# Row maxima of causal attention: 32x32 block transposes on VectorE and eight small transfers per half, in place of TensorE transposes

## The chip, the cores and the metric

One core of one Trainium2 chip runs the whole program. The metric is the device time of one execution in microseconds (us); lower is better. The engines are PE (TensorE, matrix products; PEld is its weight load), DVE (VectorE), ACT (ScalarE), POOL (GpSimd) and SP (SyncE, which here only issues DMA transfers). "ACTq" and "SPq" are DMA issues on the queues of ACT and SP.

## The reference, cut to what matters

The input has 32 sequences of 376 tokens (375 and one of padding) with 256 features. Three layers follow one another: a token mixer (a causal filter of 32 taps and two projections), causal attention with 16 heads of 16 features, and a mixture of experts. Only the attention is touched:

```python
q = (x @ wq + bq).reshape(b, s, h, hd).transpose(0, 2, 1, 3)
k = (x @ wk + bk).reshape(b, s, h, hd).transpose(0, 2, 1, 3)
...
scores = jnp.einsum('bhqd,bhkd->bhqk', q, k) / jnp.sqrt(jnp.float32(hd))
scores = jnp.where(causal, scores, -jnp.inf)
weights = jax.nn.softmax(scores, axis=-1)
attn = jnp.einsum('bhqk,bhkd->bhqd', weights, v)
```

The softmax subtracts, for each query and head, the largest score of its row. The change is about how that maximum gets from where it is found to where it is used.

## The kernel before

**Three phases.** The attention phase works through 32 sequences and takes about the first 1320 us. The routing phase and the pages phase (the experts) follow; the change doesn't touch them.

**A step.** The attention phase is software-pipelined: step b attends to sequence b, finds the row maxima of sequence b+1, makes queries and keys (the "front") for sequence b+2, mixes b+3 and finishes b-1. A step has 28 units, n = 0 to 27, in four groups of heads (g = n // 7); half 0 of the heads are units 0 to 13, half 1 units 14 to 27. In each unit PE makes one bank of scores with queries on the partitions (for the maxima of sequence b+1, line 584) and one with keys on the partitions (for the exponentials of sequence b, line 618). Between them it does the dense products of the step, each at a unit written out by hand: `hid` at 1 and 2, `nT` at 9 and 10, q at 13 and 14, k at 17 and 18, `out` at 22 and 23, `conv` at 24 and 25, `val` at 6 and 27. Every engine runs its own program in its own order and waits on semaphores. A dense product lies in one of two banks, taken in turn; the next but one product waits until ACT (`take_hi`) and DVE (`take_lo`) have read it.

**The way of the maxima.** DVE reduces each bank of scores along the keys and writes minus the maximum to `neg_max` (line 830), queries on the partitions. The second pass has keys on the partitions and queries along the columns, and wants the maximum inside the product: `k_rows` holds two rows of ones, and `q_rows` gets two rows with the high and the low part of minus the maximum, so that the product comes out as score minus maximum. So the maxima must be turned:

- `max_T` (PE): three transposes per half (line 566) of `neg_max`, 8 heads by 376 queries, into a dense bank. Half 1 is turned at unit 5 of the next step, half 0 at unit 20.
- `take_hi` (ACT, unit 5 or 20) writes the high part, `take_lo` (DVE, unit 6 or 21) the low part, to `maxT`, 8 rows of 376.
- `max_rows` (SP, line 1088): four transfers per half, each of four rows of 1504 B, from `maxT` to the one row of `q_rows` that it fills.
- `open_exp` (PE): unit 0 waits until half 0 has landed in `q_rows`, unit 14 until half 1 has.

**SP's order in a step:** `max_rows` of half 1; the rows of half 0 of q (8 transfers) and k (6), waiting for q and k of this step; `max_rows` of half 0; `store` (2); `load_x` (2, waits for `conv1`); the rows of half 1 of q (8, waits for the exponentials of unit 27) and k (6). SP issues one after another.

**Clears.** At units 9 and 11 ACT issues one transfer each of 816 KB of zeros to DRAM (`x_sorted`, `y_sorted`; line 746), which the phases behind need.

Of the kernel before, what the change touches and what calls it, by code (L numbers as in the profile page):

```python
# [24 lines left out]
F32 = mybir.dt.float32  # L25
# [8 lines left out]
P = 128  # L34
# [60 lines left out]
def attention_phase(nc, sem, sh, front, experts, h2_dram, x_sorted, y_sorted, pages_cleared,  # L95
# [7 lines left out]
    ROWS = 3 * sh.HD  # L103

    with ExitStack() as ctx:
# [44 lines left out]
        q_rows = [sb(f"q_rows{p}", [P, 8, S], F32R) for p in range(2)]  # L150
# [3 lines left out]
        maxT = [sb(f"maxT_{s}", [8, 2, S], F32R) for s in ("hi", "lo")]  # L154
# [28 lines left out]
        max_taken = sem("max_taken")  # L183
        exp_scores = sem("exp_scores")
# [42 lines left out]
        with nc.Block() as block:  # L227
# [75 lines left out]

            @block.tensor
# [88 lines left out]
        DENSE = 16  # L393

        class Step:
# [14 lines left out]
            @staticmethod  # L410
            def names(b):

                mix, front, maxima, attend, finish = (0 <= b + d < B for d in (3, 2, 1, 0, -1))
                return (["hid0", "hid1"] * front + ["maxT1"] * attend + ["val0"] * maxima
                        + ["nT0", "nT1", "q0", "q1", "k0", "k1"] * front + ["maxT0"] * maxima
                        + ["out0", "out1"] * finish + ["conv0", "conv1"] * mix + ["val1"] * maxima)
# [60 lines left out]
        with nc.Block() as block:  # L477

            @block.tensor
            def _(eng):  # L480
# [80 lines left out]
                def max_T(st, half, shift):  # L561

                    ps = open_bank(st, f"maxT{half}")
                    eng.wait_ge(max_taken, st.at(shift, GROUPS * UNITS, 2 * UNITS * (half + 1)))
                    for t in range(NT):
                        last = eng.transpose(ps[0:8, t * P:t * P + T[t]], neg_max[0:T[t], t, half, :],
                                             ident[0:T[t], 0:T[t]])
                    close(last)

# [34 lines left out]
                def open_exp(st, g, u):  # L604
                    n = g * UNITS + u
                    if u == 0 and g % 2 == 0:
                        eng.wait_ge(max_loaded[st.b % 2][g // 2], st.turn(0, 64, 64))
# [54 lines left out]
                def step(st):  # L662
                    for n in range(GROUPS * UNITS):
# [10 lines left out]
                        if n == 5 and st.attend:  # L674
                            max_T(st, 1, 0)
# [8 lines left out]
                        if n == 20 and st.maxima:  # L684
                            max_T(st, 0, 1)
# [12 lines left out]
            def _(eng):  # L698
# [64 lines left out]
                def step(st):  # L763
                    opens = isinstance(st.i, int) and st.b == -2
                    for n in range(GROUPS * UNITS):
# [9 lines left out]
                        if n == 5 and st.attend:  # L775
                            take_hi(st, "maxT1", maxT[0][0:8, 1, :], 8)
# [19 lines left out]
                        if n == 20 and st.maxima:  # L796
                            take_hi(st, "maxT0", maxT[0][0:8, 0, :], 8)
# [5 lines left out]
            def _(eng):  # L803
# [3 lines left out]
                HI = ["maxT1", "nT0", "nT1", "q0", "q1", "k0", "k1", "maxT0", "conv0", "conv1"]  # L807
# [13 lines left out]
                def maxima(st, g, u):  # L821
# [8 lines left out]
                    eng.tensor_reduce(dst, src, AX.X, ALU.max, negate=True).then_inc(max_taken, 1)  # L830

# [60 lines left out]
                def step(st):  # L892
                    for n in range(GROUPS * UNITS):
# [7 lines left out]
                        if n == 6 and st.attend:  # L901
                            take_lo(st, "maxT1", maxT[1][0:8, 1, :], maxT[0][0:8, 1, :], 8)
# [13 lines left out]
                        if n == 21 and st.maxima:  # L916
                            take_lo(st, "maxT0", maxT[1][0:8, 0, :], maxT[0][0:8, 0, :], 8)
# [116 lines left out]
            def _(eng):  # L1034
# [15 lines left out]
                def rows(st, half, name):  # L1050
# [11 lines left out]
                    for c in range(2):  # L1062
                        for n, part in enumerate(order):
                            eng.dma_start(dst[par][64 * c + 16 * n:64 * c + 16 * n + 16, 4 * half:4 * half + 4, :]
# [3 lines left out]
                    if name == "q":  # L1068
                        for c in range(2):

                            at, slots = 64 * c + ROWS, slice(4 * half, 4 * half + 4)
                            eng.dma_start(q_rows[par][at:at + 2, slots, :].bitcast(F32),
                                          q_rows[par][at + 2:at + 4, slots, :].bitcast(F32)
# [6 lines left out]
                def max_rows(st, half, shift):  # L1080

                    par = (st.b + shift) % 2
                    _, k = st.product(f"maxT{half}")
                    eng.wait_ge(dense_read, k + 1)
                    for c in range(2):
                        for part in range(2):
                            row_ = 64 * c + ROWS + part
                            eng.dma_start(q_rows[par][row_:row_ + 1, 4 * half:4 * half + 4, :].bitcast(F32),
# [1200 lines left out]
```

## Time and profile before

| | |
|---|---|
| median of 3 runs | 2006.88 us (1999.67 to 2010.14) |
| profiled execution, first to last instruction | 2006.0 us |
| PE busy over the span | 1780.7 us, 89% |
| DVE busy over the span | 1414.0 us, 70% |
| ACT, POOL busy over the span | 1006.7 us, 1057.2 us |
| attention phase, first to last score product | about 58 to 1297 us |
| DMA packets over the span | 214515, 291.09 MB |

The profiled execution's record gives its span and no further time around it; it lies 0.9 us under the median of the runs. A busy share says how long an engine had something in it; since matrix products overlap in PE, a busy PE isn't at its peak. Idle time of an engine is put down to what ended it.

### The profile page before, as it was taken

The numbers are of one execution on the slowest core, as the hardware profiler recorded it, in microseconds if no ns is written. First come the engines' busy times: TensorE is split into PE (matmuls) and PEld (weight loads), VectorE is DVE, ScalarE is ACT, GpSimd is POOL, SyncE is SP. The second block draws the span as 40 slices with busy tenths as digits, with TensorE's granted clock in tenths as the row PEclk, the third lists the DMA queues.
The fourth block names the chain that finished last, engine by engine and source line by source line (L and its number), as shares of the span: only waits on it lengthen the run. The fifth ranks groups of instructions, "written<-read, shape, count | busy, mean of one in ns | idle before, by whom it ended". The sixth has DMA issues, their size and how long they took to land. (4 is left out here: it accounts for less than half of the span.)

```text
span 2006.0 us, 49812 instructions
## 1 busy us (share of the span) xinstructions
PE 1780.7 (89%) x14801; PEld 1389.7 (69%) x14802; DVE 1414.0 (70%) x3857; ACT 1006.7 (50%) x2112; POOL 1057.2 (53%) x1443
## 2 busy tenths in 40 slices
PE   4899999999999999999999998848889984988883
PEld 4667777777777777777777776447777774977773
DVE  3468788788788788788788787357888872355554
ACT  1156556556556556656656656532443431544441
POOL 4034555555555555555555554525667663266666
PEclk7689999999999999999999999768999997999997
DMA  2434343343334334334334333222333335799996
GB/s 74 75 111 138 121 131 136 121 129 137 120 128 138 120 126 140 120 125 141 120 125 142 119 113 136 67 82 84 117 108 125 111 112 157 236 329 325 325 317 222
DMA packets 214515, 291.09 MB, mean 145 GB/s; under 512 B 44854, under 2 KB 176666, under 8 KB 214426
## 3 DMA queue, kind: packets, MB, share of 16 engines
q1 hardware_dynamic: 178010, 186.11, 30.1%
q0 software_dynamic: 18048, 49.31, 7.7%
q10 hardware_dynamic: 18368, 54.64, 7.1%
q8 instruction: 38, 0.62, 0.1%
q14 instruction: 51, 0.42, 0.1%
HBM read 83.25 MB, written 129.69 MB: 106 GB/s over the span
## 5 line engine op out<-in xcount | busy, mean ns | idle before, releaser
L830 DVE TENSOR_REDUCE neg_max<-bank 120x1 f32<-120x376 f32 (+2 forms) x896 | 522.3, 596 | 215.5 <-PE bank L584 208.6
L739 ACT ACTIVATE probs<-bank 128x376 f32<-128x376 f32 (+2 forms) x896 | 454.7, 522 | 281.7 <-PE bank L618 270.6
L584 PE MATMUL bank<-k_rows,q_rows 64*128 64x128 f32 (+2 forms) x1536 | 412.0, 342 | 31.5 <-ACT probs L739 27.7
L618 PE MATMUL bank<-q_rows,k_rows 64*120 64x120 f32 (+2 forms) x1536 | 397.6, 343 | 4.2 <-ACT probs L739 4.2
L949 POOL TENSOR_SCALAR_AFFINE_SELECT probs<-probs 128x512 f32<-128x512 f32 (+1 forms) x384 | 233.9, 628 | 241.5 <-ACT probs L739 241.5
L601 PE MATMUL bank<-causal,own_row 64*120 64x120 bf16 (+4 forms) x1792 | 293.1, 244 | 12.1 <-DMA k_rows<-k_flat_hi 8.2
L584 PEld LDWEIGHTS bank<-k_rows,q_rows 64*128 64x128 f32 (+1 forms) x1536 | 240.9, 189 | 51.0 <-ACT probs L739 46.0
L2171 POOL DMA_INDIRECT y_got<-y_sorted,p_route x188 | 183.0, 973 | 122.1 <-issue 117.9
L1815 POOL DMA_INDIRECT x_sorted<-r_normed,route x188 | 183.8, 978 | 103.2 <-DVE route L1662 50.1
L618 PEld LDWEIGHTS bank<-q_rows,k_rows 64*128 64x128 f32 (+1 forms) x1536 | 230.5, 184 | 9.1 <-ACT probs L739 6.6
L601 PEld LDWEIGHTS bank<-causal,own_row 64*128 64x128 bf16 (+2 forms) x1792 | 149.8, 115 | 125.1 <-issue 56.0
L654 PE MATMUL bank<-probs,val 128*32 128x376 f32 (+2 forms) x3072 | 193.3, 385 | 2.6 <-POOL probs L949 2.6
L890 DVE RECIPROCAL recip<-sums 128x94 f32<-128x94 f32 x256 | 186.0, 729 | 0.1
L654 PEld LDWEIGHTS bank<-probs,val 128*32 128x32 f32 (+1 forms) x3072 | 88.7, 112 | 97.5 <-issue 73.1
L975 POOL TENSOR_TENSOR attn_raw<-attn_raw,recip 128x376 f32<-128x376 f32 x64 | 63.8, 996 | 144.7 <-DVE recip L890 144.7
L1364 PE MATMUL rbank<-shared_down,r_hidden 128*128 128x256 f32 x376 | 93.4, 391 | 28.2 <-DVE base L1518 28.2
L2129 DVE SCALAR_TENSOR_TENSOR base<-y_got,p_route,base 128x256 f32 (+1 forms) x94 | 41.4, 482 | 100.9 <-DMA y_got<-y_sorted,p_route 100.9
L1002 POOL TENSOR_TENSOR resid<-hid,bias_o 128x256 f32<-128x256 f32 (+1 forms) x96 | 67.7, 733 | 72.4 <-DVE out_rows L874 72.4
L2010 PE MATMUL pbank<-w_gate_up,xT 128*128 x816 | 105.5, 285 | 0.0
L2010 PEld LDWEIGHTS pbank<-w_gate_up,xT 128*128 128x128 f32 x816 | 99.4, 199 | 1.1 <-issue 0.5
L1364 PEld LDWEIGHTS rbank<-shared_down,r_hidden 128*128 128x128 f32 x376 | 67.8, 190 | 41.4 <-DVE base L1518 33.9
L955 POOL TENSOR_SCALAR var_eps<-moments 128x3 f32<-128x3 f32 x32 | 7.4, 233 | 167.1 <-DVE moments L850 167.1
(226 smaller groups left out, 4176.3 us busy)
## 6 DMA issues: line engine op xcount, KB each, us to landing
x_sorted<-zeros ACTq DMA_DIRECT2D x32, 816.0 KB, 4.0
y_sorted<-zeros ACTq DMA_DIRECT2D x32, 816.0 KB, 4.4
x_rows<-x_sorted SPq DMA_DIRECT2D x51, 512.0 KB, 6.2
y_sorted<-p_y_rows SPq DMA_DIRECT2D x51, 512.0 KB
q_rows<-q_flat_hi SPq DMA_DIRECT2D x256, 94.0 KB
k_rows<-k_flat_hi SPq DMA_DIRECT2D x248, 94.0 KB
q_rows<-q_flat_lo SPq DMA_DIRECT2D x128, 94.0 KB
out_dram<-base SPq DMA_DIRECT2D x47, 256.0 KB
```

Of the source, the lines that this page charges most:

```text
L584: last = eng.matmul(ps[0:T[t], m * w:(m + 1) * w], q[rows, slot, t * P:t * P + T[t]], k[rows, slot, 0:w], start=False, stop=(m == len(head ...
L601: eng.matmul(dst, own_row[group, h, 0:d], causal[group, h, 0:m, first:d], start=(h == 0), stop=False, skip_group_check=True)
L618: last = eng.matmul(ps[0:T[t], m * w:(m + 1) * w], k[64 * c:64 * c + 64, slot, t * P:t * P + T[t]], q[64 * c:64 * c + 64, slot, t * P:S], ...
L654: last = eng.matmul(bank_pv[32 * j:32 * j + 32, t * P:S], val[par][0:kk, t, 4 * (g // 2) + j, 32 * e:32 * e + 32], probs[g % 2][0:kk, j, O ...
L739: eng.activation(probs[g % 2][0:T[t], first:first + len(heads), OFF[t]:OFF[t] + w], bank_exp[n % 2][0:T[t], 0:len(heads) * w].rearrange("k ...
L830: eng.tensor_reduce(dst, src, AX.X, ALU.max, negate=True).then_inc(max_taken, 1)
L890: eng.reciprocal(recip[:, cols], sums[:, cols]).then_inc(recip_done, 1)
L949: eng.affine_select(out=blk, in_=blk, compare_op=ALU.is_ge, fill=0.0, base=0, pattern=[[0, 4], [1, d]], channel_multiplier=-1).then_inc(pr ...
L1364: last = eng.matmul(bank_y[t // 2][:, t % 2 * D:(t % 2 + 1) * D], hidden[c][:, t * P:(t + 1) * P], experts.down[:, c, :], start=(c == 0 an ...
L1815: eng.indirect_dma_start(x_sorted, at, normed[st.b % 4][:, t, :], None)\
L2010: last = eng.matmul(bank_gu[par][:, a * 2 * MR:(a + 1) * 2 * MR], xT[par][a // 2][:, k, a % 2 * P:(a % 2 + 1) * P], routed.gate_up[:, k, e ...
L2171: eng.indirect_dma_start(y_got[ring][:, t, k, :], None, y_sorted, at)\
```

## The change

The PE transposes, the copies by ACT and DVE, `maxT` and two of the 16 dense products of a step go. In their place DVE, after its own maximum of unit 0 (half 1) or unit 14 (half 0), writes the high and low parts of the maxima side by side into `max_parts`, 32 columns per query tile, and turns them in blocks of 32x32 into `max_turned`. A query's place is then (tile, block of 32, column in it), and the blocks of one tile lie on four groups of 32 partitions; so SP carries them to `q_rows` in eight transfers per half, each from 8 partitions to two rows, in runs of 32 numbers (128 B), 24 runs in each. `q_rows` grows from 376 to 384 columns. Half 0 is turned six units earlier than before, half 1 five units earlier. SP's order is unchanged.

```diff
-        q_rows = [sb(f"q_rows{p}", [P, 8, S], F32R) for p in range(2)]
+        q_rows = [sb(f"q_rows{p}", [P, 8, SPAN], F32R) for p in range(2)]
...
-        maxT = [sb(f"maxT_{s}", [8, 2, S], F32R) for s in ("hi", "lo")]
+        max_parts = [sb(f"max_parts{h}", [P, NT, 32], F32R) for h in range(2)]
+        max_turned = [sb(f"max_turned{h}", [P, NT, 32], F32R) for h in range(2)]
...
-        DENSE = 16
+        DENSE = 14
...
-                def max_T(st, half, shift):
-
-                    ps = open_bank(st, f"maxT{half}")
-                    eng.wait_ge(max_taken, st.at(shift, GROUPS * UNITS, 2 * UNITS * (half + 1)))
-                    for t in range(NT):
-                        last = eng.transpose(ps[0:8, t * P:t * P + T[t]], neg_max[0:T[t], t, half, :],
-                                             ident[0:T[t], 0:T[t]])
-                    close(last)
...
-                        eng.wait_ge(max_loaded[st.b % 2][g // 2], st.turn(0, 64, 64))
+                        eng.wait_ge(max_loaded[st.b % 2][g // 2], st.turn(0, 128, 128))
...
-                        if n == 5 and st.attend:
-                            max_T(st, 1, 0)
...
-                        if n == 20 and st.maxima:
-                            max_T(st, 0, 1)
...
-                        if n == 5 and st.attend:
-                            take_hi(st, "maxT1", maxT[0][0:8, 1, :], 8)
...
-                        if n == 20 and st.maxima:
-                            take_hi(st, "maxT0", maxT[0][0:8, 0, :], 8)
...
+                def turn_maxima(st, half, shift):
+
+                    parts = max_parts[half][:, :, 0:16].rearrange("q t (c s m) -> q t c s m", c=2, s=2)
+                    whole = neg_max[:, :, half, :].rearrange("q t (c m) -> q t c m", c=2)
+                    done = st.at(shift, 2, half + 1)
+                    eng.wait_ge(max_taken, st.at(shift, GROUPS * UNITS, 2 * UNITS * (half + 1)))
+                    eng.tensor_copy(parts[:, :, :, 0, :], whole).then_inc(max_hi, 1)
+                    eng.wait_ge(max_hi, done)
+                    eng.tensor_tensor(parts[:, :, :, 1, :], whole, parts[:, :, :, 0, :].bitcast(F32), ALU.subtract)\
+                        .then_inc(max_lo, 1)
+                    eng.wait_ge(max_lo, done)
+                    eng.transpose(max_turned[half][:, :, :].rearrange("q t i -> q (t i)").bitcast(F32),
+                                  max_parts[half][:, :, :].rearrange("q t i -> q (t i)").bitcast(F32)).then_inc(max_turns, 1)
...
-                        if n == 6 and st.attend:
-                            take_lo(st, "maxT1", maxT[1][0:8, 1, :], maxT[0][0:8, 1, :], 8)
+                        if n == 0 and st.attend:
+                            turn_maxima(st, 1, 0)
+                        if n == 14 and st.maxima:
+                            turn_maxima(st, 0, 1)
...
                 def max_rows(st, half, shift):
 
                     par = (st.b + shift) % 2
-                    _, k = st.product(f"maxT{half}")
-                    eng.wait_ge(dense_read, k + 1)
+                    wait_alone(eng, max_turns, st.at(shift, 2, half + 1), passed_sp)
                     for c in range(2):
-                        for part in range(2):
-                            row_ = 64 * c + ROWS + part
-                            eng.dma_start(q_rows[par][row_:row_ + 1, 4 * half:4 * half + 4, :].bitcast(F32),
-                                          maxT[part][4 * c:4 * c + 4, half, :].bitcast(F32)).then_inc(max_loaded[par][half], 16)
+                        rows_ = q_rows[par][64 * c + ROWS:64 * c + ROWS + 2, 4 * half:4 * half + 4, :].bitcast(F32)\
+                            .rearrange("s m (t b i) -> s m t b i", b=4, i=32)
+                        for b in range(4):
+                            eng.dma_start(rows_[:, :, :, b, :],
+                                          max_turned[half][32 * b + 8 * c:32 * b + 8 * c + 8, :, :].bitcast(F32)
+                                          ).then_inc(max_loaded[par][half], 16)
```

The rest of the diff clears `neg_max` and `max_parts` once at the start, adds three semaphores and drops the two names from the lists that number the dense products.

## Rows read from the trace of the kernel before

**Rows 1.** The page: span, and busy time of each engine

```profile
span 2006.0 us, 49812 instructions
...
PE 1780.7 (89%) x14801; PEld 1389.7 (69%) x14802; DVE 1414.0 (70%) x3857; ACT 1006.7 (50%) x2112; POOL 1057.2 (53%) x1443
```

**Rows 2.** Windows: stretch and length, busy by engine, PE clock, DMA share, GB/s

```profile
241.00:1184.00 943.00, 917.04 (x8750) 676.96 (x8748) 759.99 (x1625) 580.91 (x1225) 489.37 (x725) 1.00 0.39 128
```

**Rows 3.** Timeline of PE, units 5 to 9 of one step (start, length in us)

```profile
713.92 0.49 PE L566 MATMUL bank<-ident,neg_max 128*8 128x128 f32 x3
714.34 0.26 PE L601 MATMUL bank<-causal,own_row 64*120 64x120 bf16 x1
...
718.51 0.38 PE L584 MATMUL bank<-k_rows,q_rows 64*128 64x256 f32 x1 [0.54 <-ACT probs L739]
```

**Rows 4.** Timeline of ACT, unit 6 of the same step

```profile
716.42 1.58 ACT L714 ACTIVATE normed<-hid,row_shift_by,rstd 128x256 f32<-128x256 f32 x3 [0.22 <-POOL row_shift_by L963]
```

**Rows 5.** Waits from 200 to 1200 us: total, times, longest (us)

```profile
ACT normed L714 <- POOL row_shift_by L963: 6.5, 26, 0.3
...
PEld bank L515 <- DVE out_rows L874: 7.6, 25, 0.3
```

**Rows 6.** Timeline of POOL, unit 20 of the same step

```profile
734.91 0.64 POOL L949 TENSOR_SCALAR_AFFINE_SELECT probs<-probs 128x512 f32<-128x512 f32 x1 [1.38 <-ACT probs L739]
```

**Rows 7.** Groups of DVE: smallest operand, and the 32-partition shuffle

```profile
L1561 DVE TENSOR_TENSOR shifted<-top 128x8 f32<-128x8 f32 x23 | 3.6, 158 | 0.0
...
L884 DVE STREAM_SHUFFLE sums<-sums_swapped 128x376 f32<-128x376 f32 x64 | 37.6, 588 | 0.3
```

**Rows 8.** Timeline of DVE, the maximum of unit 2 in the next step

```profile
748.19 0.69 DVE L830 TENSOR_REDUCE neg_max<-bank 128x2 f32<-128x512 f32 x1 [0.77 <-PE bank L584]
```

**Rows 9.** Timeline of SP's queue, late part of the step

```profile
738.03 0.68 SPq L1088 DMA_DIRECT2D q_rows<-maxT_hi  x1
...
740.05 0.57 SPq L1088 DMA_DIRECT2D q_rows<-maxT_lo  x1
741.00 0.42 SPq L1104 DMA_DIRECT2D h_dram<-out_rows  x1
...
743.01 0.41 SPq L1045 DMA_DIRECT2D x_in<-in_x_dram  x1
...
745.10 1.29 SPq L1064 DMA_DIRECT2D q_rows<-q_flat_hi  x2
...
753.58 0.59 SPq L1064 DMA_DIRECT2D k_rows<-k_flat_hi  x1
```

**Rows 10.** Timeline of SP's queue near the end of the phase

```profile
1274.94 0.58 SPq L1088 DMA_DIRECT2D q_rows<-maxT_hi  x1
```

**Rows 11.** Transfers from 1274.5 to 1279.5 us, in 40 slices

```profile
GB/s 0 0 0 0 0 0 0 0 0 0 0 0 0 24 24 0 0 0 24 24 0 0 0 24 24 0 0 0 24 24 0 366 418 418 418 287 339 261 392 366
```

**Rows 12.** Timeline of PE: first exponential products of units 0 and 14

```profile
744.38 0.42 PE L618 MATMUL bank<-q_rows,k_rows 64*120 64x120 f32 x2
...
762.03 0.42 PE L618 MATMUL bank<-q_rows,k_rows 64*120 64x120 f32 x2
```

**Rows 13.** Timeline of ACT's queue: second clear of the same step

```profile
758.80 0.55 ACTq L746 DMA_DIRECT2D y_sorted<-zeros  x1
```

**Rows 14.** Transfers from 756.5 to 764.5 us: issues, size, us to landing

```profile
y_sorted<-zeros ACTq DMA_DIRECT2D x1, 816.0 KB, 4.4
```

**Rows 15.** Timeline of ACT's queue, step with the late rows

```profile
1244.75 0.54 ACTq L746 DMA_DIRECT2D y_sorted<-zeros  x1
```

**Rows 16.** Timeline of SP's queue in that step

```profile
1246.32 1.35 SPq L1088 DMA_DIRECT2D q_rows<-maxT_lo  x1
```

**Rows 17.** Timeline of PE in that step, unit 14

```profile
1250.26 0.33 PE L584 MATMUL bank<-k_rows,q_rows 64*128 64x128 f32 x1 [3.31 <-DMA q_rows<-maxT_lo]
```

**Rows 18.** Windows around an idle stretch of PE: columns as in rows 2

```profile
113.50:115.20 1.70, 0.04 (x1) 0.00 (x0) 1.38 (x4) 1.70 (x5) 1.37 (x3) 1.00 0.02 7
...
117.20:120.40 3.20, 3.20 (x28) 1.25 (x28) 1.52 (x4) 1.01 (x3) 0.00 (x0) 0.50 1.02 406
```

More of the change, by code:

```diff
@@ L103, in attention_phase @@
     ROWS = 3 * sh.HD
+    SPAN = NT * P
     with ExitStack() as ctx:
@@ L183, in attention_phase @@
         max_taken = sem("max_taken")
+        max_hi = sem("max_hi")
+        max_lo = sem("max_lo")
+        max_turns = sem("max_turns")
         exp_scores = sem("exp_scores")
@@ L302, in _ @@
                 eng.memset(moments[:, :, :], 1.0)
+                eng.memset(neg_max[:, :, :, :], 0.0)
+                for h in range(2):
+                    eng.memset(max_parts[h][:, :, :].bitcast(F32), 0.0)
             @block.tensor
@@ L413, in names @@
                 mix, front, maxima, attend, finish = (0 <= b + d < B for d in (3, 2, 1, 0, -1))
-                return (["hid0", "hid1"] * front + ["maxT1"] * attend + ["val0"] * maxima
-                        + ["nT0", "nT1", "q0", "q1", "k0", "k1"] * front + ["maxT0"] * maxima
+                return (["hid0", "hid1"] * front + ["val0"] * maxima
+                        + ["nT0", "nT1", "q0", "q1", "k0", "k1"] * front
                         + ["out0", "out1"] * finish + ["conv0", "conv1"] * mix + ["val1"] * maxima)
@@ L806, in _ @@
                 HALF_1_AT, HALF_0_AT = (10, 11, 12, 13, 16), (22, 24, 25, 26, 27)
-                HI = ["maxT1", "nT0", "nT1", "q0", "q1", "k0", "k1", "maxT0", "conv0", "conv1"]
+                HI = ["nT0", "nT1", "q0", "q1", "k0", "k1", "conv0", "conv1"]
                 def take_lo(st, name, dst, hi, rows=P, bias=None):
@@ L915, in step @@
                             take_lo(st, f"k{j}", k_flat[1][:, j, :], k_flat[0][:, j, :], bias=bias_k[:, j:j + 1])
-                        if n == 21 and st.maxima:
-                            take_lo(st, "maxT0", maxT[1][0:8, 0, :], maxT[0][0:8, 0, :], 8)
                         if st.attend and n in HALF_0_AT:
@@ L1063, in rows @@
                         for n, part in enumerate(order):
-                            eng.dma_start(dst[par][64 * c + 16 * n:64 * c + 16 * n + 16, 4 * half:4 * half + 4, :]
+                            eng.dma_start(dst[par][64 * c + 16 * n:64 * c + 16 * n + 16, 4 * half:4 * half + 4, 0:S]
                                           .bitcast(F32),
@@ L1071, in rows @@
                             at, slots = 64 * c + ROWS, slice(4 * half, 4 * half + 4)
-                            eng.dma_start(q_rows[par][at:at + 2, slots, :].bitcast(F32),
-                                          q_rows[par][at + 2:at + 4, slots, :].bitcast(F32)
+                            eng.dma_start(q_rows[par][at:at + 2, slots, 0:S].bitcast(F32),
+                                          q_rows[par][at + 2:at + 4, slots, 0:S].bitcast(F32)
                                           ).then_inc(rows_loaded[par][half], 16)
```

## The prediction

> **What bounds the kernel now.** I read the page first: PE is busy for 89% of the span, DVE for 70% [rows 1]. By windows, the even part of the attention phase shows PE busy for 917 of 943 us at a clock of 1.00 [rows 2], so 26 us of it are waits of PE; this is 25 steps of 37.7 us, about 1 us of waiting in each. The first thought is that PE sets the pace and every product taken from it is won. So I looked in the timeline of one step for where PE waits and on what that wait depends, then at the queue that gets the new transfers, and last at the moments when PE needs what they bring.
>
> Units are called by their n. The steps repeat closely enough that one stands for all: unit 0's first exponential product starts at 744.38, unit 14's at 762.03 [rows 12].
>
> **PE's work removed: nothing gained.** The three transposes of one half hold PE from 713.92 until the next unit starts at 714.34, so 0.42 us; 64 such groups in 32 steps would be 27 us. What is behind each is what counts.
>
> Half 1, unit 5. At unit 9 PE waits 0.54 us for ACT's exponentials until 718.51 [rows 3]. ACT is late there because `normalise` at unit 6 starts only at 716.42 and takes 1.58, and it had itself idled 0.22 for `row_shift_by` of POOL [rows 4]; this wait is there in 26 of 26 steps of the even part [rows 5]. POOL gets its statistics from DVE, which has them from `hid` at units 1 and 2. This chain leaves PE at unit 2 and comes back at unit 9, and the transposes at unit 5 stand between the two. If they go, PE reaches unit 9 0.42 earlier and waits 0.96 instead of 0.54. The same holds for ACT's `take_hi` at unit 5: ACT would idle longer before `normalise`.
>
> Half 0, unit 20. `conv0` at unit 24 needs the bank that `out0` leaves, and PE's weight load for it waits for DVE's `out_rows` in 25 steps, 7.6 us in all [rows 5]. DVE's program is held there by its shuffle of the sums, this by POOL's `join`, and POOL's last mask before `join` starts at 734.91 after 1.38 idle, as soon as ACT has the exponential of unit 20 [rows 6]. In ACT's order that exponential comes before `take_hi` of the maxima, and it hangs on `k1` of unit 18 and the `keep` of unit 19. Again the chain passes outside of the transposes, and the 0.42 goes into the wait at unit 24. I take 0 for both; the other end is 0.84 per step.
>
> **DVE: nothing.** Per half a subtraction over 376 columns goes and three small instructions come. The smallest operands take 0.16 each [rows 7]; the copy and the subtraction have 24 columns, the block transpose 96. For the last the trace has no row; it lies between 0.16 and the 0.59 of the shuffle over 376 columns [rows 7], and I take 0.25, nearer to the small one, as 96 is nearer to 8 than to 376. With two waits for a result just written, some 0.05 each, the three come to 0.7 (0.6 to 1.0). Behind them in DVE's queue stands the maximum of unit 1, and behind that the one of unit 2, before which DVE idles 0.77 for PE [rows 8]. The 0.7 fits in. In unit 14 the next are `take_lo` of q0 and the maximum of unit 15, with a similar idle time. Without this cover it would be 0.25 us too late at `hid`, which feeds the chain of half 1: 8 us in all, at most. POOL has nothing new but one memset before the loop.
>
> **SP's queue: half 0 just fits.** Four transfers start between 738.03 and 740.05, so one every 0.67 [rows 9]. A small transfer into SBUF lands about 1.4 after its issue starts: one issued at 1274.94 [rows 10] moves in the 14th and 15th of the slices of 0.125 us from 1274.5, so until 1276.4 [rows 11]. In the old kernel the last lands at 741.5. With eight it starts at 738.03 + 7 x 0.67 = 742.7 and lands at 744.1; PE wants it at 744.38. Each new transfer has 24 runs of 128 B where the old one had 4 of 1504 B. The trace has no such transfer. An issue takes 0.41 to 0.68 whatever it carries [rows 9], and I keep 0.67; the bounds are 0.61 a transfer (0.57 and a gap), and 0.72 with 0.3 more to land, which gives 743.7 and 744.8. So the wait is 0 (0 to 0.4).
>
> **Half 1 doesn't fit.** The four additional issues, 2.7 us, push `store`, `load_x` and the rows of half 1 of q and k. Between 741.00 and 745.10 SP has four issues of about 0.4 and a gap of some 0.2 after each, 2.4 of 4.1 us [rows 9]; it can absorb 1.7 and passes on 1.0. The last transfer of k then starts at 754.6 instead of 753.58 [rows 9] and the first of the maxima at 755.2 (half 1 is turned at unit 0, long before). The eighth starts at 755.2 + 4.7 = 759.9. In quiet it would land at 761.3, in time for 762.03.
>
> But it isn't quiet. ACT issues the second clear at 758.80 [rows 13] and it lands 4.4 later, at 763.2 [rows 14]; the first was issued some 1.8 earlier, and while clears move the transfer engines carry about 400 GB/s without a gap [rows 11, 18]. The old kernel has its last row of half 1 issued and landed before that. One step, near the end of the phase, shows what happens when it hasn't: the clear was issued at 1244.75 [rows 15], the last row of maxima at 1246.32, and this issue alone took 1.35 in place of 0.57 [rows 16, 9]. PE stood for 3.31 us and went on at 1250.26 [rows 17], 3.9 after the issue of the row and 5.5 after that of the clear, so with the clear and not before it.
>
> The Trainium skill has a rule for it (DMA: Bandwidth & Descriptors, section "Queues, rings and completion order"): a transfer's count on its semaphore is written only after every earlier write of the same transfer engine, of other queues too. Rows 17 agree; by the rule alone the wait would last until the clear lands, 763.2, or 1.2 us in each step and 2043 us for the kernel.
>
> From the rows I put the wait at unit 14 between 1.2 (758.80 + 4.4 against 762.03) and 2.3 (758.80 + 5.5), and take 1.5, nearer to the even step than to the odd one. What hangs on PE there, `q1`, k and SP's next round, moves with it, so it isn't recovered. About 30 steps have both a clear and the full order of SP.
>
> **Sum.** 0 (PE) + 0 (DVE) + 0 (half 0) + 30 x 1.5 = 45 us on the profiled 2006.0, which is 2051; the median is 0.9 above that execution, so 2052.
>
> **Rivals.**
> 1. The wait also costs clock. After PE idled for 1.70 us its granted clock was 0.50 from 117.2 to 120.4, that is 1.2 of 2.4 GHz, against 1.00 before [rows 18]; this costs 1.6 us of the 3.2. With 1.5 of wait it is 3.1 in each step, 93 in all: 2100. For it: the idle time has nearly the same length. Against it: shorter waits of 0.54 in each step leave 1.00 [rows 2, 3].
> 2. No change. The rows of the maxima are a few hundred bytes, pass between the pieces of the clear, and land 1.4 after their issue. Then nothing waits, and what PE saves goes into its waits: 2007. For it: 0.7 us of slack in quiet. Against it: the one collision of the trace.
> 3. Faster. The transfers land in time and PE's 0.84 per step is won, because its waits at units 9 and 24 are shorter than I read them or move with the rest: 32 x 0.84 = 27, so 1980. It decides if PE's idle time at unit 9 stays at 0.5. For it: PE is 97% busy [rows 2]. Against it: both chains pass outside of what is removed.
>
> **Chances.** My forecast 0.42, clock 0.22, no change 0.18, faster 0.18. A measurement of this kernel tells some 0.5% (10 us) from no change. Slower by over 0.5% is 0.64, within it 0.18, faster 0.18. The likeliest case alone spans 2036 to 2076 (30 x 1.0 and 30 x 2.3). The range reaches to 1988, into the faster case, and to 2105, beyond the clock's.
>
> **What would show it.** In the profile after: the step longer by about 1.5 us; waits of PE at line 618 or 584 for DMA into `q_rows` at unit 14, more than 1 us, in nearly every step, which now hardly exist; eight issues of 0.6 to 0.7 us on SP per half, those beside the clears longer; PE's waits at units 9 and 24 about 0.4 longer; three DVE instructions of 0.7 together; the granted clock of the even part, 1.00 if the forecast holds and lower if the first rival does. Wrong it would be if PE's wait for the maxima is absent, or if issues of the new shape take much more or less than 0.67.

## The result and the profile after

The changed kernel takes 2101.36 us (median of 4 runs, 2099.09 to 2109.57) and the kernel before, in the same session, 2005.84 (4 runs). The ratio is 1.0474, with a 95% interval from 1.0441 to 1.0508: 95 us slower.

The page of the changed kernel, span and busy times, against [rows 1]:

```profile
span 2100.3 us, 49634 instructions
...
PE 1832.7 (87%) x14609; PEld 1407.9 (67%) x14610; DVE 1434.0 (68%) x3985; ACT 993.3 (47%) x2048; POOL 1055.8 (50%) x1446
```

PE has 192 matmuls fewer by program and is busy 52 us longer. A busy time that grows while work is taken away points at the clock. The windows of the same stretch as in [rows 2] show it:

```profile
241.00:1184.00 943.00, 888.35 (x7953) 638.99 (x7951) 718.58 (x1597) 529.49 (x1088) 450.77 (x669) 0.92 0.40 120
```

The granted clock is 0.92 where it was 1.00, and PE idles 54.7 us where it idled 26.0 (943.00 less its busy time). ACT starts one clear of `x_sorted` in each step, and the first and the last of the 26 steps that the kernel's loop makes give the length of a step. Before:

```profile
L746 ACTq MOVE x_sorted<-zeros x26: 29/29/38, 153.2 to 1096.5; - x26
```

After:

```profile
L742 ACTq MOVE x_sorted<-zeros x26: 29/29/38, 158.5 to 1176.6; - x26
```

These are 943.3 and 1018.1 us for 25 steps, 37.73 and 40.72 each. The step is 2.99 us longer. Idle time of PE is 1.32 of that (26.0 us over 25.0 steps before, 54.7 over 23.2 after). The other 1.67 is PE's busy time, which grew although work had gone: 0.84 a step by the row of the transposes, 0.45 by the busy times of e12 and e13 below. So I estimate that the clock costs 2.1 to 2.5. Behind the phase nothing is lost: from the first clear to the last of all 32 it is 92.3 us more (1253.5 against 1161.2), nearly the whole difference.

Where PE idles, and what the clock does after it, is in the timeline of PE. In one step, at unit 9 (in [rows 3] the wait here was 0.54), and its windows, columns as in [rows 2]:

```profile
319.66 0.38 PE L584 MATMUL bank<-k_rows,q_rows 64*128 64x256 f32 x1 [1.26 <-ACT probs L735]
```
```profile
319.60:320.00 0.40, 0.34 (x4) 0.30 (x4) 0.13 (x1) 0.40 (x2) 0.40 (x1) 1.00 0.20 23
320.20:320.90 0.70, 0.70 (x3) 0.40 (x3) 0.69 (x1) 0.58 (x1) 0.70 (x2) 0.50 0.11 15
320.90:322.00 1.10, 1.10 (x7) 0.76 (x7) 0.18 (x1) 0.63 (x2) 1.10 (x3) 0.50 0.38 151
322.00:326.00 4.00, 4.00 (x33) 1.71 (x32) 2.89 (x7) 1.31 (x3) 0.31 (x1) 0.50 0.75 297
```

PE stands for 1.26 us, resumes at full clock, and within 0.6 us runs at 0.50, which is the lower of its two levels of 1.2 and 2.4 GHz, until 326 and beyond. In this step there is no wait for a transfer at unit 14. In the step of sequence 15, one ahead of the one that [rows 3, 4, 6] come from, it is the other way round. The pause at unit 9 is the same, the clock stays up, and the forecast wait for the maxima comes at unit 14 (timeline of PE, then the windows behind it):

```profile
726.80 0.38 PE L584 MATMUL bank<-k_rows,q_rows 64*128 64x256 f32 x1 [1.25 <-ACT probs L735]
...
734.47 0.32 PE L584 MATMUL bank<-k_rows,q_rows 64*128 64x128 f32 x1 [1.42 <-DMA q_rows<-max_turned]
```
```profile
736.00:744.00 8.00, 8.00 (x54) 5.35 (x53) 4.85 (x10) 3.28 (x6) 3.61 (x5) 0.57 0.28 73
```

So two pauses compete. In windows of 1 us from 241 to 1184, I count 23 pauses at unit 9 (1.15 to 1.26 us); behind 19 of them the clock falls within 3 us. The four waits for the maxima (1.41 to 1.44) stand in exactly the other four steps, and the clock falls behind two of them. The waits from 200 to 1200 us:

```profile
PE bank L584 <- ACT probs L735: 48.7, 94, 1.3
PE bank L584 <- DMA q_rows<-max_turned: 7.8, 5, 2.1
...
ACT normed L710 <- POOL row_shift_by L969: 16.9, 24, 0.8
```

The last of these was 6.5 us in [rows 5].

VectorE's turn of half 1 at unit 0, and what GpSimd does beside it:

```profile
717.16 0.64 DVE L830 CAST max_parts<-neg_max 128x24 fp32r<-128x24 f32 x1
717.84 0.18 DVE L832 TENSOR_TENSOR max_parts<-neg_max,max_parts 128x24 fp32r<-128x24 f32 x1
718.05 0.28 DVE L835 STREAM_TRANSPOSE max_turned<-max_parts 128x96 f32<-128x96 f32 x1
```
```profile
716.78 0.99 POOL L981 TENSOR_TENSOR attn_raw<-attn_raw,recip 128x376 f32<-128x376 f32 x1 [0.49 <-DVE recip L896]
```

The copy of 24 columns takes 0.64 us and ends with GpSimd's instruction, at about 717.8. The block transpose takes 0.28. It is not this step alone: 28 of the 64 copies meet this instruction of GpSimd (line 981), and they take 0.5 to 0.7; the 34 that meet none take 0.17 at most.

### The profile page after: what moved, and what is told of

Read it like the earlier page. It is cut to its first block and busy times, and to the rows that moved or that the text cites. A ratio compares the mean times of both kernels' runs of the same rounds, so it can differ in the third digit from the quotient of the medians.

```text
span 2100.3 us, 49634 instructions
## 1 busy us (share of the span) xinstructions
PE 1832.7 (87%) x14609; PEld 1407.9 (67%) x14610; DVE 1434.0 (68%) x3985; ACT 993.3 (47%) x2048; POOL 1055.8 (50%) x1446
## 5 line engine op out<-in xcount | busy, mean ns | idle before, releaser
L584 PE MATMUL bank<-k_rows,q_rows 64*128 64x128 f32 (+2 forms) x1536 | 433.8, 359 | 78.7 <-ACT probs L735 62.1
L618 PE MATMUL bank<-q_rows,k_rows 64*120 64x120 f32 (+2 forms) x1536 | 408.4, 355 | 3.8 <-ACT probs L735 3.8
L584 PEld LDWEIGHTS bank<-k_rows,q_rows 64*128 64x128 f32 (+1 forms) x1536 | 256.8, 201 | 118.6 <-ACT probs L735 89.9
L601 PE MATMUL bank<-causal,own_row 64*120 64x120 bf16 (+4 forms) x1792 | 299.1, 253 | 12.1 <-DMA k_rows<-k_flat_hi 8.4
L618 PEld LDWEIGHTS bank<-q_rows,k_rows 64*128 64x128 f32 (+1 forms) x1536 | 238.7, 192 | 9.2 <-ACT probs L735 6.4
L601 PEld LDWEIGHTS bank<-causal,own_row 64*128 64x128 bf16 (+2 forms) x1792 | 160.1, 122 | 122.8 <-issue 56.8
L654 PE MATMUL bank<-probs,val 128*32 128x376 f32 (+2 forms) x3072 | 221.5, 429 | 2.6 <-POOL probs L955 2.6
L654 PEld LDWEIGHTS bank<-probs,val 128*32 128x32 f32 (+1 forms) x3072 | 95.8, 121 | 119.3 <-issue 100.0
```

Of the source, the lines that this page charges most:

```text
L584: last = eng.matmul(ps[0:T[t], m * w:(m + 1) * w], q[rows, slot, t * P:t * P + T[t]], k[rows, slot, 0:w], start=False, stop=(m == len(head ...
L601: eng.matmul(dst, own_row[group, h, 0:d], causal[group, h, 0:m, first:d], start=(h == 0), stop=False, skip_group_check=True)
L618: last = eng.matmul(ps[0:T[t], m * w:(m + 1) * w], k[64 * c:64 * c + 64, slot, t * P:t * P + T[t]], q[64 * c:64 * c + 64, slot, t * P:S], ...
L654: last = eng.matmul(bank_pv[32 * j:32 * j + 32, t * P:S], val[par][0:kk, t, 4 * (g // 2) + j, 32 * e:32 * e + 32], probs[g % 2][0:kk, j, O ...
```

## The experiments

The trace of after suggested a theory, T: PE's longer pause at unit 9 brings the clock down. Against it stood the forecast's own, R: the transfers of half 1 come late because of the clears. The experiments that follow also asked what makes the pause longer, whether missing work matters by itself, and whether the removed products are worth anything at full clock.

| kernel | ratio to before (95%) | step, us | pause at unit 9 (median) | pauses followed by a fall | clock 241 to 1184 |
|---|---|---|---|---|---|
| before | 1 | 37.73 | 0.56 | 0 of 25 | 1.00 |
| after | 1.0474 (1.0441 to 1.0508) | 40.72 | 1.24 | 19 of 23 | 0.92 |
| e1 clears later | 1.0379 (1.0351 to 1.0406) | 40.24 | 1.24 | 19 of 23 | 0.93 |
| e2 e1, idle products | 1.0094 (1.006 to 1.0127) | 38.00 | 0.68 | 0 of 25 | 1.00 |
| e3 e1, turn at unit 4 | 1.0322 (1.028 to 1.0364) | 40.21 | 1.12 | 19 of 23 | 0.93 |
| e4 before, fewer products | 1.0011 (0.9983 to 1.004) | 37.90 | 0.78 | 2 of 25 | 1.00 |
| e5 e2, clears back | 1.0569 (1.0524 to 1.0615) | 41.36 | 0.69 | 0 of 22 | 0.94 |
| e6 before, norm late | 1.0203 (1.0161 to 1.0245) | 39.16 | 1.18 | 11 of 24 | 0.98 |
| e7 normalise at 7 to 9 | 1.092 (1.0879 to 1.0962) | 43.31 | two waits | - | 0.89 |
| e8 before, the same | 1.0827 (1.078 to 1.0873) | 43.04 | two waits | - | 0.91 |
| e9 e3, normalise at 6 to 8 | 1.0271 (1.0213 to 1.0329) | 39.46 | 0.95 | 14 of 24 | 0.95 |
| e10 before, the same | 1.0147 (1.009 to 1.0203) | 38.78 | 0.95 | 9 of 24 | 0.98 |
| e11 e1, products behind | 1.0135 (1.0071 to 1.0199) | 38.62 | 1.23 | 7 of 24 | 0.99 |
| e12 e3, chain early | 1.011 (1.0075 to 1.0146) | 37.96 | none over 0.5 | - | 1.00 |
| e13 before, chain early | 0.9999 (0.9962 to 1.0036) | 37.72 | none over 0.4 | - | 1.00 |
| e14 e1, one group of idle products | 1.0052 (1.0016 to 1.0089) | 38.03 | 0.69 | 0 of 24 | 1.00 |

A step is worked out as above, from the 26 clears; a fall is a window of 1 us under 0.9 that begins within 3 us of the pause. e9 to e14 ran on two other chips, where the kernel before takes 2187.85 and 2172.06 us (before had 2005.64 and 2006.84 in the sessions of the others). The time that those chips add lies behind 1184 us, in the stage after this one: e13's step of 37.72 is that of before. So these six are read by ratio and by step. The falls are counted in one profiled execution of each kernel, and they are not independent draws. In the changed kernel the time from the end of the pause to the fall grows from 0.2 to 0.9 us over six steps in a row, shown here by the first and the last; in e1 the four steps without a fall come in two pairs, and in e11 the falls come in every third or fourth step. So it also matters when a pause comes, and such a count is not a probability.

```profile
278.82:279.00 0.18, 0.18 (x2) 0.18 (x4) 0.11 (x1) 0.18 (x1) 0.18 (x1) 1.00 0.77 150
279.10:280.10 1.00, 1.00 (x7) 0.52 (x5) 0.63 (x1) 0.72 (x2) 1.00 (x2) 0.50 0.07 8
...
482.95:483.80 0.85, 0.85 (x7) 0.61 (x7) 0.50 (x2) 0.70 (x2) 0.85 (x2) 1.00 0.15 21
484.00:485.00 1.00, 1.00 (x6) 0.68 (x7) 0.42 (x2) 0.76 (x3) 1.00 (x3) 0.50 0.15 51
```

**e1, clears later.** 

```diff
-                        if n == 9 and st.attend:
+                        if n == 14 and st.attend:
                             clear_pages(st, x_sorted)
-                        if n == 11 and st.attend:
+                        if n == 15 and st.attend:
                             clear_pages(st, y_sorted)
```

> The changed kernel with the two clears issued at units 14 and 15 instead of 9 and 11, so that no bulk transfer runs beside the eight small ones of half 1. The forecast's theory (the transfers of half 1 come late because of the clears, TensorE waits for them at unit 14, and the rest of the loss follows from that wait): the wait for the transfers goes and so does the loss, 2005 to 2015 us. The theory formed from the trace of after (TensorE's idle time ahead of unit 9 grew from 0.56 to about 1.2 us in every step, and the granted clock falls to one half for 4 to 7 us about 1 us later, in 24 of 26 steps): the waits for the transfers (16.6 us in the run) go, but the idle time of 1.2 us and the low clock behind it stay in nearly every step, 2075 to 2100 us, mean granted clock from 241 to 1184 us still about 0.93.

2085.79 us. No wait for the transfers is left in the stretch, and 79 us of the loss are still there. The clock falls behind the pause at unit 9 as often as before, 19 of 23. R alone can't be the cause.

**e2, idle products at units 5 and 20.**

```diff
+                def filler(st, name):
+                    ps = open_bank(st, name)
+                    for t in range(NT):
+                        eng.transpose(ps[0:8, t * P:t * P + T[t]], ident[0:T[t], 0:8], ident[0:T[t], 0:T[t]])
...
+                        if n == 5 and st.maxima:
+                            filler(st, "val0")
...
+                        if n == 20 and st.finish:
+                            filler(st, "out0")
```

> e1 with TensorE's removed work put back without its purpose: three transposes of 8 columns each at units 5 and 20, into the bank that the next dense product opens anyway; nobody reads them. If the idle time of unit 9 is what brings the clock down, it shrinks here by the 0.42 us that the three products took, from 1.2 to about 0.8 us (the other 0.25 us, the norm chain that starts later on VectorE, stays): with the clock up 2005 to 2020 us, and if 0.8 us are still enough to bring it down, 2070 to 2100 as e1. The theory that VectorE's or SP's added work costs the time expects no difference from e1, whatever TensorE does.

2027.73 us, with more work than e1 and 58 us less time. That is 8 us above T's value for a clock that stays up. VectorE's turn and all the transfers are still in it, so with no clear beside them they cost no more than the 0.9% that is left (1.3% at the end of its interval). What this rest is made of no run shows; 0.27 x 31 = 8 us of it are in the step. The timeline of its PE at unit 9, its windows, and its SP queue, where the eight transfers take 5.40 us:

```profile
460.60 0.38 PE L590 MATMUL bank<-k_rows,q_rows 64*128 64x256 f32 x1 [0.69 <-ACT probs L745]
```
```profile
241.00:1184.00 943.00, 915.27 (x8685) 667.26 (x8683) 766.66 (x1711) 563.71 (x1165) 486.53 (x722) 1.00 0.48 128
```
```profile
460.19 5.40 SPq L1104 DMA_DIRECT2D q_rows<-max_turned  x8
```

**e3, half 1 turned at unit 4.** In `turn_maxima(st, 1, 0)` on VectorE, `n == 0` becomes `n == 4`.

> e1 with half 1 turned at unit 4 instead of unit 0, behind the norm statistics on VectorE instead of ahead of them: the norm chain starts as early as before, so the normalise of ScalarE waits 0.2 us for GpSimd's shift again and not 0.73, and TensorE's idle time at unit 9 is about 0.98 us (0.56 plus the 0.42 of the removed products) instead of 1.2. The eight transfers are issued some 7 us later but still land ahead of unit 14. If the length of that idle time decides over the clock: between 2010 and 2075 us, less than e1 in any case. If the products' removal alone does it: as e1, 2075 to 2100. If the turn's place is nothing to it: as e1.

2076.26 us. The copy never takes more than 0.17 us here (its line, min/median/max):

```profile
L830 DVE CAST max_parts<-neg_max x64: 108/165/168, 79.5 to 1338.5; 128x24 fp32r<-128x24 f32 x64
```

Beside the copies at unit 4 GpSimd runs only instructions of 128x3. The place of the turn costs 0.12 us of pause (1.24 to 1.12), which is also what separates e2 from before (0.68 to 0.56). The missing products give 0.56 of it (e1 against e2), more than the 0.42 that they took. The 9.5 us less than e1 are from the first and last steps of the phase: in the even part the step is 40.21 against 40.24. The shorter pause did not help there, and the clock fell as often. The time lies 1 us above what was expected of a shorter stretch, inside the expectation "as e1".

**e4, before with two of three transposes of half 1 less.**

```diff
-                    for t in range(NT):
+                    for t in (range(NT) if half == 0 else (2,)):
```

> The kernel before with only the third of the three transposes of half 1 at unit 5; it leaves out the maxima of the first two query tiles of half 1. Nothing of VectorE's turn and none of the new transfers is in it. TensorE's idle time at unit 9 grows by the two products (0.28 of 0.42 us), from 0.56 to about 0.84 us. If work taken from TensorE ahead of its wait brings the clock down by itself: slower than before, 2030 to 2090 us, with stretches at clock 0.50 behind unit 9. If 0.84 us of idle time are too few for that, or if the loss comes from VectorE's or SP's new work: no difference, 2000 to 2010 us.

2008.06 us, no difference: at a pause of 0.78 the clock fell in 2 steps of 25. What is taken away is not won, and not lost either as long as the pause stays short.

**e5, e2 with the clears back at 9 and 11.**

> e2 with the clears back at units 9 and 11: the changed kernel as it is, plus three idle transposes at units 5 and 20. Only TensorE's work is put back; the clears still meet the transfers of half 1. The forecast's theory (the transfers come 1.5 us late at unit 14 in 30 steps) expects 1.5 us more in every step than e2, 2065 to 2075 us. The theory of the idle time ahead of unit 9 expects the clock up and most of the loss gone, 2027 to 2045 us, with a wait for the transfers in single steps.

2123.79 us, the opposite of what T expected and 49 us over R's upper value. The waits of its PE from 241 to 1184 us, and one of them in the timeline with the windows behind it:

```profile
PE bank L590 <- DMA q_rows<-max_turned: 32.0, 22, 1.6
PE bank L590 <- ACT probs L745: 17.4, 37, 0.7
```
```profile
486.28 0.32 PE L590 MATMUL bank<-k_rows,q_rows 64*128 64x128 f32 x1 [1.40 <-DMA q_rows<-max_turned]
```
```profile
478.70:486.00 7.30, 6.18 (x58) 3.78 (x58) 6.32 (x13) 4.81 (x11) 3.23 (x5) 1.00 0.62 236
487.20:491.00 3.80, 3.80 (x23) 3.19 (x21) 2.69 (x8) 1.80 (x4) 0.00 (x0) 0.55 0.00 0
```

Once the clock survives unit 9, the maxima of half 1 are late at unit 14 in 22 steps of 22, by 1.38 to 1.57 us, and all 22 are followed by a fall. The queues of the same step:

```profile
478.09 6.83 SPq L1104 DMA_DIRECT2D q_rows<-max_turned  x8
```
```profile
481.16 0.55 ACTq L752 DMA_DIRECT2D y_sorted<-zeros  x1
```

Beside the clears the eight issues take 6.83 us in place of 5.40. The last of them ends at 484.92, the clear lands 4.3 after its issue, at 485.5, and PE goes on at 486.28, 0.8 behind the clear. So the slower issues are part of the delay; how much of it is theirs and how much is the landing behind the clear no run separates. Against e2 the step is 3.36 longer, at the same work: by the windows of both, 1.25 of that is idle time of PE and 2.1 is busy time, which at the same work is the clock (e5's window):

```profile
241.00:1184.00 943.00, 888.87 (x7976) 649.61 (x7974) 703.43 (x1569) 515.79 (x1068) 445.26 (x661) 0.94 0.40 116
```

So T is only half of it. In the changed kernel R is hidden in 19 of 23 steps: after a fall at unit 9 TensorE gets to unit 14 later, and ACT issues the second clear 2.8 to 4.1 us behind the pause where it is 2.5 in the four steps without a fall. The pause at unit 9 taken away, the one at unit 14 comes forth; the other way round the one at unit 9 stays, as in e1. Both must go, as in e2.

**e6, the norm chain late in the kernel before.**

```diff
+                    eng.tensor_copy(pad[:, :], zeros[:, 0:480])
                     eng.tensor_scalar(shift_by[:, :], scaled_mean[:, :], -1.0, None, ALU.mult).then_inc(shift_done, 1)
```

> The kernel before with nothing removed from TensorE and nothing of the change in it: a copy of 128x480 zeros on GpSimd, whose nearest row is the 128x376 copy of 0.50 us, ahead of the shift that ScalarE's normalise waits for. TensorE's idle time at unit 9 should grow from 0.56 to about 1.2 us. If the length of this idle time decides over the clock: clock 0.50 behind unit 9 in nearly every step and 2090 to 2110 us, some 3 us in each step and 0.65 us of them the idle time itself. If it takes TensorE's lost work: only the idle time itself, 26 times 0.65, 2020 to 2030 us, at clock 1.00.

2048.92 us, between both expectations. The pause alone, with nothing of the change, is followed by a fall of the clock, but in 11 of 24 steps. The timeline of PE and the windows at such a step:

```profile
474.23 0.38 PE L585 MATMUL bank<-k_rows,q_rows 64*128 64x256 f32 x1 [1.21 <-ACT probs L740]
```
```profile
474.20:475.90 1.70, 1.67 (x14) 1.19 (x14) 1.03 (x3) 1.31 (x3) 1.70 (x3) 1.00 0.02 7
476.00:480.00 4.00, 4.00 (x38) 1.92 (x36) 2.69 (x7) 1.33 (x4) 0.89 (x2) 0.58 0.93 378
```

**e11, e2 with the idle products of unit 5 at unit 10.** `filler(st, "nT1")` at unit 10 takes the place of `filler(st, "val0")` at unit 5.

> e2 with the three idle transposes of unit 5 moved to unit 10, right behind the idle time instead of ahead of it: the same work for TensorE in each step as in e2 and in the kernel before, but the idle time at unit 9 stays at 1.2 us. If the length of that stretch decides, as e1 (2075 to 2090 us); if the amount of work decides, as e2 (2020 to 2035 us); between them, as in the kernel with the late shift (2049 us), if both have a part.

The ratio is 1.0135. The pause stays at 1.23, and the clock falls behind 7 of 24. On the first chips this ratio would be 2034 us, so it fits "as e2", if at its end: the length of the pause alone doesn't decide, and the same work behind the pause in place of ahead of it wins back most of the loss. Together with e6 the falls are fewer where the work is in place: 19 of 23 in each of the changed kernel, e1 and e3, against 7 and 11 of 24, at pauses of 1.12 to 1.24. Whether that comes from the work itself or from the moment at which the pauses then come is not shown.

**e7 and e8, normalise at units 7 to 9.** ScalarE's three instructions, one each behind the exponentials of units 7, 8 and 9, `nT0` and `nT1` a unit later; in e1 and in the kernel before.

> e1 with ScalarE's three normalise instructions behind the exponentials of units 7, 8 and 9, one each, where they stood together ahead of that of unit 7, and the two products that read them at units 10 and 11 instead of 9 and 10. By the theory of the idle time the stretch of 1.2 us at unit 9 breaks up into pieces of under 0.8 us, the clock stays up, and TensorE's removed 0.42 us become a gain in each step: 1985 to 2010 us. If the idle time only moves to unit 10 as one piece: as e1, 2075 to 2090.

> The same spread of the normalise instructions and the same two products a unit later, in the kernel before: the control for e7. Its idle time of 0.56 us at unit 9 goes, at most 0.56 us in each of 27 steps, so 1990 to 2006 us. If e7 is faster than this one the change is worth its removed products; if it is not, the change buys nothing here even at full clock.

Both much slower, 2191.86 and 2170.83 us, and both expectations missed. The waits of PE in e7:

```profile
PE bank L503 <- DVE normedT_lo L807: 27.7, 22, 1.4
...
PE bank L549 <- ACT normed L710: 22.2, 22, 1.0
```

PE now waits 1.0 for the last third of `normed` and again 1.1 to 1.4 for the low part of `nT1`. I had looked at ACT's order alone and not at who needs the products a unit later.

**e9 and e10, normalise at units 6 to 8**, the products left at 9 and 10; in e3 and in before.

> e3 (clears at units 14 and 15, half 1 turned at unit 4) with ScalarE's three normalise instructions behind the exponentials of units 6, 7 and 8, one each, and both products that read them left at units 9 and 10. The one stretch of 1.12 us should break up into pieces of at most 0.5 us. If one long stretch decides over the clock: clock 1.00 between 241 and 1184 us and a time at or under that of before, 1985 to 2007 us, since 0.42 us of TensorE's work are gone in each half. If TensorE's missing work alone does it: clock still under 0.96, 2050 to 2080 us.

> The same order of the normalise instructions in the kernel before, the control for e9. Its idle time of 0.56 us goes or becomes small, at most 0.4 us in each of 27 steps: 1995 to 2007 us. If e9 is under this one, the removal of the products is a gain once nothing stops the clock; if both are the same, it is none.

The pause moved from the scores to the transposes and kept 0.95 us, so these two missed their aim as well. As a pair on one chip they point the same way as e11: the same pause is followed by a fall in 14 of 24 steps without the products, 9 of 24 with them. As single traces they don't prove it, and e9 also has the wait of 0.46 that is described under e12.

**e12 and e13, the norm chain a unit early**, in e3 and in before: `hid0`, `hid1` at units 0 and 1, their results at 1 and 2, normalise at 5 to 7. The pause at unit 9 goes.

> e3 with the norm chain one unit earlier in its whole length: the two mixing products at units 0 and 1, their results and the statistics on VectorE at 1 and 2, and ScalarE's three normalise instructions behind the exponentials of units 5, 6 and 7, one each; the products that read them stay at 9 and 10, the turn of half 1 at 4. No idle stretch of over 0.6 us should be left in the step. By the theory that the stretch stops the clock: clock 1.00 between 241 and 1184 us, and the removed 0.84 us of TensorE's work in each step become a gain, 1975 to 2003 us. By the theory that the smaller amount of work is enough to stop it: clock under 0.98, 2010 to 2070 us.

> The same earlier norm chain in the kernel before, the control for e12: its one idle stretch of 0.56 us goes, 1990 to 2003 us. If e12 is 10 us or more under it, the removal of the products pays once the stretch is gone; if they agree within 0.3 per cent it doesn't.

Clock 1.00 in both, as expected. But e12 is 1.1% slower than before, and e13 equal to it. Windows and waits of PE from 241 to 1184 us, e13 first:

```profile
241.00:1184.00 943.00, 919.62 (x8751) 679.36 (x8750) 760.39 (x1625) 582.58 (x1225) 490.93 (x726) 1.00 0.39 128
```
```profile
PE bank L584 <- ACT probs L739: 15.3, 75, 0.3
```
```profile
241.00:1184.00 943.00, 902.70 (x8537) 654.03 (x8539) 756.46 (x1710) 560.15 (x1166) 485.18 (x717) 1.00 0.48 128
```
```profile
PE bank L584 <- ACT probs L735: 26.9, 97, 0.5
PE bank L584 <- DMA q_rows<-max_turned: 4.1, 14, 0.9
```

In each step PE is busy 0.45 us less in e12 (902.70 over 24.85 steps against 919.62 over 25.0) and idle 0.69 more. The removed work turned into waits for ScalarE's exponentials and for the maxima. One of 0.46 comes in every step of e12, e14, e1, e3 and the changed kernel, which all lack the products of unit 20, at unit 22 just ahead of `out0`; before, e13 and e2 don't have it. In e12:

```profile
712.37 0.38 PE L584 MATMUL bank<-k_rows,q_rows 64*128 64x256 f32 x1 [0.46 <-ACT probs L735]
```

Of e12's 1.1%, 24 us, the step explains 0.24 x 31 = 7 us. Between the first and the last of all 32 clears it is 12 us over e13 (1170.9 against 1158.8, from the timelines of ACT's queue), so 5 more are in the first and last steps; the other 12 lie outside of the clears, most of them in the steps that fill the pipeline (the first clear is issued at 132.7 against 117.1, part of it because it stands five units later). I have no cause for them.

**e14, e2 with the products of unit 5 only.**

> e2 without the idle transposes of unit 20, so that only the three at unit 5 are put back: the stretch at unit 9 stays at 0.7 us as in e2, and TensorE's work is 0.42 us less in each step. If the stretch decides: as e2, 2020 to 2035 us. If the amount of work has a part of its own at this length too: clock stops in some steps, 2035 to 2070 us.

The ratio is 1.0052, the step 38.03 against e2's 38.00, the clock 1.00. At the short pause 0.42 us less work neither stops the clock nor shortens the step.

## Why the prediction was wrong

**The step that failed** is the clock at nothing. The forecast let every wait cost only its own length, since "shorter waits of 0.54 in each step leave 1.00", and put the case in which a wait costs clock second, at 2100 us and 0.22. In its place the runs showed a clock of 0.92, which costs 2.1 to 2.5 us a step, and idle time that grew by 1.32. The forecast itself lengthened the pause at unit 9 from 0.54 to 0.96 and did not ask what this does to the clock. The rows bounded it: 0.54 left the clock up and 1.70 was followed by a fall [rows 3, 18], so a pause that goes from the one towards the other had to be priced at both ends. And the pause of 1.70 in [rows 18] is this very wait, at unit 9 of an early step, which the forecast didn't look up (kernel before):

```profile
115.24 0.38 PE L584 MATMUL bank<-k_rows,q_rows 64*128 64x256 f32 x1 [1.70 <-ACT probs L739]
```

- *PE's work removed: 0.* Right as a gain: e14, e4 and e12 show that the products are worth nothing at full clock. Wrong as a cost: the pause became 1.24 and not 0.96 (0.56 for the products by e1 and e2, 0.12 for the turn; why the products of 0.42 give 0.56 is open), and a fall of the clock follows. In unit 24 the wait of PE's weight load for `out_rows` did not grow (7.9 us in all against 7.6); the wait that unit 20's products left behind is the one of 0.46 for an exponential, at unit 22.
- *VectorE: 0.7 us, hidden.* At unit 14 it is that. At unit 0 it is 1.17 (717.16 to 718.33), because the copy stands behind GpSimd's instruction. The cover was too short, as the other end said (0.25 too late); 0.12 of it reached PE's pause. The Trainium skill (SBUF — State Buffer, "Who interferes with whom") has copies and casts among the instructions that can claim the port pair shared with GpSimd, and the later of two waits for the whole of the earlier. The trace agrees: 0.64 us beside GpSimd's instruction, 0.17 in e3 at unit 4.
- *SP, half 0: fits.* Right: no wait at unit 0 in the even part. An issue takes 0.62 us (median of 512), and in quiet one starts every 0.68 (eight in 5.40, e2), against 0.67.
- *SP, half 1: 1.5 us of wait at unit 14.* The size is right where PE comes on time, 1.38 to 1.57 in e5 and 1.42 in the step above, and so is the meeting with the clears; the eight issues themselves take 6.83 there, where the forecast had 5.3 (4.7 to the start of the eighth and 0.6 for it). There the first transfer started at 726.26, 11.1 us behind unit 0, which starts at 715.12 (10.8 by the forecast), and PE went on 19.35 behind unit 0 (19.1). In the changed kernel itself only 4 of 23 steps show it, where the forecast had it in 30, because the earlier fall of the clock takes its place. By the forecast's own sign ("if PE's wait for the maxima is absent") that was wrong.
- *Sum.* 45 us became 95. The first rival gave the right time, 2100, from a mechanism that is shown (a wait of that length can bring the clock down), at a place that fits few steps. That it meets the measured time so closely is luck: it priced 1.5 of idle time and 1.6 of clock, all of it at unit 14. Measured are 1.32 and 1.67 in a step, and the idle time grew by 0.68 at unit 9, 0.46 at unit 22 and only 0.25 at unit 14 (four times 1.42 over 23 steps). The rival without change is excluded by the time itself, and for the faster one nothing was won even with the clears moved and the clock at 1.00, in e12 (all products gone) and e14 (half of them). The stated span of the likeliest case began at 30 x 1.0, though the forecast's own lower bound of the wait is 1.2; that would be 2043 and not 2036.

No version beats the kernel before; e13 equals it.

What stays open: how the chance of a fall depends on the pause and on the work around it. The runs bracket it, by the median pause: no fall in any step up to 0.69 us, 2 of 25 at 0.78, 9 and 14 of 24 at 0.95, 7 to 19 of about 24 from 1.12 to 1.24, 22 of 22 at 1.44 (e5, unit 14), but 2 of 4 at 1.42 in the changed kernel.

## What to carry to other kernels

When work is taken from the engine that seems to bound a kernel, find the wait that it stood in front of, and add it to that wait. On TensorE price the longer pause with the clock: in the changed kernel the low clock behind pauses of 1.2 us cost some 2 us a step, more than anything that was removed. And when a fix doesn't help, look whether it uncovered a second pause that the first had hidden; e1 and e5 each undid one of two causes, and e2 undid both.

## What the runs showed of the hardware that I had not expected

- A pause of TensorE of 1.1 to 1.3 us, once in a step of 38 to 41 us and with TensorE busy 94 to 96% of the stretch, can be followed by a fall of the granted clock from 1.00 to 0.50, in up to 19 of 23 steps; the clock then stays there for 3 us or more, 6 to 7 in the mean (22 stretches in 943 us at a mean clock of 0.92), though TensorE is busy all the time (322 to 326 above).
- A pause of 1.12 to 1.24 us was followed by a fall more often where TensorE had 0.84 us less work in the step (19 of 23 in three kernels, against 7 and 11 of 24); whether the work or the moment of the pause does it is open.
- Small issues on SP's queue take longer while bulk transfers from another queue move: eight took 6.83 us in place of 5.40.
- A copy of 128x24 on VectorE took up to 0.92 us at the side of a GpSimd instruction, against 0.17.
